# Edge products of a graph layer: two columns per product through a block-diagonal weight, and the bias as a bf16 product

## What is computed

```
e = edge_feats @ W_e + b_e                 # 200000 x 64 times 64 x 128, plus the bias
m = relu(e + node_feats[src])              # a gathered row of x for every edge
agg = segment_sum(m, dst, num_segments=n)
h = agg + (1.0 + eps) * node_feats
z = relu(batch_norm(h @ W1 + b1))
x = layernorm(x + z @ W2 + b2)
```

## Time and profile before

| | |
|---|---|
| median of 3 runs | 3382.34 us (3381.54 to 3385.09) |
| span of the profiled execution | 3381.6 us |
| edge loop (first window's addition to the last) | about 66 to 2360 us |
| PE busy | 2729.1 us, 81% |
| PE weight loads busy | 2301.2 us, 68% |
| DVE busy | 2217.4 us, 66% |
| ACT busy | 1611.3 us, 48% |
| POOL busy | 1526.4 us, 45% |

### The profile page before, as it was taken

The page is one execution under the profiler, slowest core; times in us unless marked ns, Lnnn a source line. Parts: engine busy times, 40 slices in busy tenths (PEclk is TensorE's granted clock), DMA queues, the critical chain, the costliest instruction groups (busy, mean ns, idle before and its releaser), DMA issues.

```text
span 3381.6 us, 49409 instructions
## 1 busy us (share of the span) xinstructions
PE 2729.1 (81%) x16231; PEld 2301.2 (68%) x16231; DVE 2217.4 (66%) x4031; ACT 1611.3 (48%) x2900; POOL 1526.4 (45%) x1641
## 2 busy tenths in 40 slices
PE   4777777777777777777777778777799999999995
PEld 3666666666666666666666667666578888888884
DVE  7676666666666666666666666667778874445445
ACT  3444444444444444444444444444555554445443
POOL 6666666666666666666666666664200000000000
PEclk9767777777777777777777776777899999999998
DMA  5333333333333333333333333333323333333333
GB/s 196 106 109 110 110 109 108 109 111 112 111 109 109 108 111 112 109 112 109 108 109 112 112 110 110 109 108 98 119 98 126 149 122 127 144 138 138 127 139 96
DMA packets 145445, 394.75 MB, mean 117 GB/s; under 512 B 36829, under 2 KB 100153, under 8 KB 139817
## 3 DMA queue, kind: packets, MB, share of 16 engines
q1 hardware_dynamic: 93356, 278.06, 22.3%
q0 software_dynamic: 50176, 102.50, 13.2%
q10 hardware_dynamic: 1662, 10.97, 0.8%
HBM read 286.59 MB, written 104.80 MB: 116 GB/s over the span
## 4 chain that ended last, share of the span: by engine, by line
PE 41%; DVE 31%; another core or an unknown queue 15%; issue 9%; ACT 2%; DMA 2%; DVEq 0%; SPq 0%; POOL 0%; ACTq 0%
DVE z L1148 13%; PE psE L1008 12%; PE psA L1008 12%; PE psE L872 6%; PE psA L902 5%; DVE work L1136 4%; DVE work L1156 4%; DVE work L1155 4%; PE psS L886 3%; DVE onehot L1142 3%; DMA work<-in_edge_cols 1%; PE psA L979 1%; ACT wide L810 0%; PE psA L948 0%
## 5 line engine op out<-in xcount | busy, mean ns | idle before, releaser
L683 POOL DMA_INDIRECT work<-in_x_flat,idx x1568 | 1492.7, 952 | 837.6 <-issue 421.6
L872 PE MATMUL psE<-we,work 65*128 65x128 f32 x3136 | 707.2, 357 | 555.8 <-issue 500.4
L872 PEld LDWEIGHTS psE<-we,work 65*128 65x128 f32 x3136 | 563.6, 248 | 656.8 <-issue 627.2
L736 ACT ACTIVATE z<-psA 128x490 int32 x392 | 227.0, 579 | 1215.1 <-PE psA L902 612.7
L1148 DVE TENSOR_SCALAR z<-iota_r,key,scale 128x490 bf16<-128x490 f16 x1568 | 716.0, 520 | 0.0
L902 PE MATMUL psA<-z 128*128 128x245 bf16 x3136 | 658.1, 386 | 2.4 <-issue 2.3
L1160 DVE TENSOR_TENSOR acc<-psS,acc 128x144 f32 x196 | 60.4, 308 | 757.3 <-remote 756.7
L742 ACT ACTIVATE z<-iota_c,low 128x128 bf16<-128x128 f16 x1568 | 476.9, 390 | 0.0
L886 PEld LDWEIGHTS psS<-onehot,work 128*128 128x128 f32 x3136 | 446.5, 226 | 11.3 <-issue 3.1
L1008 PE MATMUL psE<-wide,halves 128*128 128x500 f32 (+1 forms) x2058 | 448.4, 376 | 5.8 <-ACT halves L819 5.4
L902 PEld LDWEIGHTS psA<-z 128*128 128x128 bf16 x3136 | 366.0, 136 | 124.4 <-issue 3.9
(11 more groups left out here) (165 smaller groups left out, 1792.8 us busy)
## 6 DMA issues: line engine op xcount, KB each, us to landing
counts<-adjacency SPq DMA_DIRECT2D x36, 3062.5 KB, 9.6
adjacency<-work SPq DMA_DIRECT2D x392, 245.0 KB
work<-in_edge_cols SPq DMA_DIRECT2D x196, 256.0 KB
work<-in_x_flat,idx POOLq DMA_INDIRECT x1568
counts<-adjacency SPq DMA_DIRECT2D x3, 1592.5 KB, 6.2
acc<-in_x_cols ACTq DMA_DIRECT2D x1, 3136.0 KB
xn<-in_x_rows ACTq DMA_DIRECT2D x1, 3136.0 KB, 31.3
x_spill<-xn SPq DMA_DIRECT2D x12, 256.0 KB, 2.2
```

Of the source, the lines that this page charges most:

```text
L683: gp.indirect_dma_start(gath[0:size(g), g % R, j, :], None, x_flat[:, :], bass.IndirectOffsetOnAxis(ap=idx[0:size(g), g, j:j + 1], axis=0) ...
L736: act.activation(taken[:, w % TAKEN, :, :], ring[:, bass.ds(at, 2 * HC)].rearrange("p (a n) -> p a n", a=ODD), ACT.Copy).then_inc(evac_ok, 1)
L872: mm = pe.matmul(psE0[0:n, j, :], eaT[0:FE + 1, g % RE, j, 0:n], we[:, :], start=True, stop=True)
```

## The change

Two columns of the edge features are now stacked on the 128 partitions (64 features each), so that `eaT` holds 4 pairs instead of 8 columns. The weight becomes a block-diagonal matrix of 128 x 256: the product of a pair yields the 128 outputs of its first column and the 128 of its second. The bias no longer is a 65th row. For each of the two PSUM banks one bf16 product of all-ones with `edge_bias` (128 x 512) writes it first, and two fp32 products of 256 columns are added on top. `edge_bias` holds b_e split exactly into three bf16 parts in its rows 0, 1 and 2, repeated four times, and zeros below; DVE makes it at the start from a broadcast load `be`. The edge product is one function for both forms of the loop.

```
-        we = sb("we", [FE + 1, F])
+        we = sb("we", [2 * FE, 2 * F])
+        edge_bias = sb("edge_bias", [P, 4, F], BF16)
+        be = sb("be", [P, 2, F])
+        be_parts = sb("be_parts", [P, 3, F], BF16)
...
-        eaT = work[:, 4096:4096 + RE * J * P].rearrange("p (r j e) -> p r j e", r=RE, j=J)
+        eaT = work[:, 4096:4096 + RE * HP * P].rearrange("p (r j e) -> p r j e", r=RE, j=HP)
...
-            sp.dma_start(eaT[0:FE, g % RE, :, :], edge_cols[g, :, :, :]).then_inc(ea_in[g % RE], 16)
+            sp.dma_start(eaT[:, g % RE, :, :], edge_cols[g, :, :, :]).then_inc(ea_in[g % RE], 16)
...
+        def edge_columns(pe, slot, n):
+            for half in range(2):
+                pe.matmul(psE0[0:n, 4 * half:4 * half + 4, :].rearrange("p j f -> p (j f)"), ones_b[:, 0:n],
+                          edge_bias[:, :, :].rearrange("p j f -> p (j f)"), start=True, stop=True)
+                for q in range(2 * half, 2 * half + 2):
+                    mm = pe.matmul(psE0[0:n, 2 * q:2 * q + 2, :].rearrange("p j f -> p (j f)"), eaT[:, slot, q, 0:n], we[:, :],
+                                   start=False, stop=True, skip_group_check=True)
+            return mm
...
+            act.dma_start(be[:, 0, :], be_row.partition_broadcast(P)).then_inc(be_in, 16)
             act.dma_start(we[:, :], we_rows[:, :]).then_inc(we_in, 16)
...
-            def edge_product(g, j0, j1):
-                n = size(g)
-                if j0 == 0:
-                    pe.wait_ge(ea_in[g % RE], 16 * (g // RE + 1))
-                    if g >= 1:
-                        pe.wait_ge(sum_ok, g)
-                for j in range(j0, j1):
-                    mm = pe.matmul(psE0[0:n, j, :], eaT[0:FE + 1, g % RE, j, 0:n], we[:, :], start=True, stop=True)
-                if j1 == J:
-                    mm.then_inc(edge_mm, 1)
+            def edge_product(g):
+                pe.wait_ge(ea_in[g % RE], 16 * (g // RE + 1))
+                if g >= 1:
+                    pe.wait_ge(sum_ok, g)
+                edge_columns(pe, g % RE, size(g)).then_inc(edge_mm, 1)
...
             pe.wait_ge(we_in, 16)
-            edge_product(0, 0, J)
-            edge_product(1, 0, J)
+            pe.wait_ge(edge_bias_ok, 1)
+            edge_product(0)
+            edge_product(1)
...
-            link(ve.memset(eaT[FE:FE + 1, :, :, :], 1.0))
+            ve.wait_ge(be_in, 16)
+            link(ve.tensor_copy(be_parts[:, 0, :], be[:, 0, :]))
+            link(ve.tensor_tensor(be[:, 1, :], be[:, 0, :], be_parts[:, 0, :], ALU.subtract))
+            link(ve.tensor_copy(be_parts[:, 1, :], be[:, 1, :]))
+            link(ve.tensor_tensor(be[:, 1, :], be[:, 1, :], be_parts[:, 1, :], ALU.subtract))
+            link(ve.tensor_copy(be_parts[:, 2, :], be[:, 1, :]))
+            link(ve.tensor_scalar(be[:, 1, :], be_parts[:, 0, :], ident[:, 0:1], None, ALU.mult))
+            for part in (1, 2):
+                link(ve.scalar_tensor_tensor(be[:, 1, :], be_parts[:, part, :], ident[:, part:part + 1], be[:, 1, :],
+                                             ALU.mult, ALU.add))
+            ve.tensor_copy(edge_bias[:, :, :], be[:, 1, :].unsqueeze(1).to_broadcast([P, 4, F])).then_inc(edge_bias_ok, 1)
```

More of the change, by code:

```diff
@@ L54, in cdiv, with build @@
     return -(-a // b)
-def build(nc, E, x_flat, x_rows, x_cols, src_slots, src_chunks, dst_rows, dst_slots, dst_chunks, edge_cols, we_rows, par_cols,
+def build(nc, E, x_flat, x_rows, x_cols, src_slots, src_chunks, dst_rows, dst_slots, dst_chunks, edge_cols, we_rows, be_row, par_cols,
           w1_rows, w2_rows, wg_rows, b2_row, out):
     N, F = out.shape
-    FE = edge_cols.shape[1]
+    FE = edge_cols.shape[1] // 2
     H = w1_rows.shape[1]
@@ L219, in build @@
         we_in = sem("we_in")
+        be_in = sem("be_in")
+        edge_bias_ok = sem("edge_bias_ok")
         cols_par_in = sem("cols_par_in")
@@ L433, in body @@
                 part = edge_cols[bass.ds(g, 1), :, :, :].rearrange("a k j p -> k (a j p)")
-                sp.dma_start(eaT[0:FE, 0, :, :].rearrange("k j p -> k (j p)"), part).then_inc(sem_s["ea"], 16)
+                sp.dma_start(eaT[:, 0, :, :].rearrange("k j p -> k (j p)"), part).then_inc(sem_s["ea"], 16)
             general_groups(sp, body)
@@ L450, in body @@
                 pe.wait_ge(sem_s["ea"], 16 * g + 16)
-                for j in range(J):
-                    mm = pe.matmul(psE0[0:n, j, :], eaT[0:FE + 1, 0, j, 0:n], we[:, :], start=True, stop=True)
-                mm.then_inc(sem_s["prod"], 1)
+                edge_columns(pe, 0, n).then_inc(sem_s["prod"], 1)
                 pe.wait_ge(sem_s["msg"], g + 1)
@@ L920, in _ @@
                 if s + 2 < G:
-                    edge_product(s + 2, 0, J)
+                    edge_product(s + 2)
                 for i in range(HP):
@@ L1417 @@
                 dst_chunks=dst.reshape(-1, P).T,
-                edge_cols=attr.reshape(groups, P, J, -1).transpose(0, 3, 2, 1),
-                we_rows=np.concatenate([weight["L0_gnn_W_e"], weight["L0_gnn_b_e"][None]]),
+                edge_cols=attr.reshape(groups, P, J // 2, -1).transpose(0, 3, 2, 1),
+                we_rows=np.block([[weight["L0_gnn_W_e"], np.zeros_like(weight["L0_gnn_W_e"])],
+                                  [np.zeros_like(weight["L0_gnn_W_e"]), weight["L0_gnn_W_e"]]]),
+                be_row=weight["L0_gnn_b_e"],
                 par_cols=np.concatenate([weight[k].reshape(-1, P).T for k in ("L0_gnn_b1", "L0_gnn_gamma", "L0_gnn_beta",
```

## The result

The changed kernel takes 3369.56 us (median of 5 runs, 3367.93 to 3371.29) against 3382.34 us, a ratio of 0.9963 with a 95% interval of 0.9952 to 0.9973: 12.8 us faster, 0.4 us below the range of the prediction and on the side to which it had given 0.16. A second pair of medians under the same condition gave 0.9964 (e10). Under another condition, found in the experiments, the kernel before takes 3045 us and the change gains nothing: it was 0.25% slower in one pair (e5).

What follows compares the result with a forecast made beforehand. POOL's chain of eight gathers and some 2.1 us of waiting was taken to bound the loop. Span 3381.6 + 0 + 0.5 (start) + 0.7 (median over span) = 3382.8, rounded 3383 us; range 3370 to 3425.

Steps and rivals of the forecast that it cites:

- POOL's chain sets the period, PE does not: Edge loop: POOL's eight gathers plus some 2.1 us of waiting set the step of about 11.8 us, not PE.
- No burst, no hold: Edge loop: where POOL's gathers stand still or have ended, PE's edge product runs unbroken, in 3.75 or 1.94 us.
- The edge product, "I take 0": Edge loop: PE's work grows 0.2 to 0.6 us a step but lies under 4.7 us of hold, so 0 us.
- the hold: Edge loop: stretch in which PE issues nearly one record at a time and `win_mm` arrives 4.7 us late.
- rival 1: The hold depends on PE's instruction form or number: one 0.7 us break less per step, 134 us, 3249 us; chance 0.15.
- Sizes of the product: Edge product on PE: 2.1 us for 1.9 at the high clock, 4.3 for 3.75 at the low one.
- Rival 2: PE sets the loop's period and the longer edge product costs 38 to 115 us, 3421 to 3498 us; chance 0.07.
- 4.7 us of hold: Edge loop: time `win_mm` comes late at DVE after the window's end on PE, taken as cover for the edge product.
- The edge transfer, 0: Edge feature load: same 256 KB on 128 partitions; landing 1 us earlier or later only moves the product's start, 0 us.
- The start, +0.5: Before the loop: 2.9 us of added DVE operations are covered by idle time; POOL's chain moves -1 to +2, taken +0.5 us.
- The end, 0: Loop end and after: DVE awaits no edge product, later instructions are the same; clock phase -2.8 to +2, taken 0 us.
- The signs of being right: Trace: bursts every 11.8 us after 2.1 us idle, DVE idle about 4 us, product 2.1 to 4.3, first addition about 66.

Runs made afterwards that it cites:

- e10: The changed kernel itself on another chip, against the kernel before, with the hold: 0.9964 (kernel before 3382.25 us).
- e5: The changed kernel itself once more, against the kernel before, without the hold: 3051.84 for 3043.46 us, 1.0025.
- e8: The kernel before with seven gathers a step in place of eight from the fifth group on: 0.9209.
- e13: The changed kernel, edge product varied by 24-step stretches: eight narrow products, no bias, behind two or four chunk pairs, issued twice; 3376.60 us in one run.
- e16: The changed kernel, edge product in stretches of 36, 20 or 12 records and different forms: 3401.47 us, kernel before 3410.76 us, one run each.
- e12: The kernel before, varied by 24-step stretches: product moved, issued twice or three times, one column of eight, seven gathers; 3448.04 us in one run.
- e4: The kernel before with each edge product issued twice, without the hold: 0.9992 of a kernel before at 3045.6 us.
- e14: The changed kernel with two memsets of acc moved from POOL to ACT and a DVE sum moved to POOL behind the loop: 0.9964, without the hold.
- e15: The kernel before with two memsets of acc moved from POOL to ACT and a DVE sum moved to POOL behind the loop: 0.9966, without the hold.
- e6: The kernel before itself, run for its trace, without the hold: profiled span 3044.2 us, loop period 10.10 us.

## Why the prediction was wrong

**POOL's chain sets the period, PE does not: right.** e8 and the seven-gather stretch (10.44 for 11.83 us: one gather of 1.25 and 0.14 of the wait) show it under both conditions. "No burst, no hold" is weaker than it was put: the product read as unbroken in the earlier trace rows, at 171.78, runs while POOL gathers again, one every 1.25 us from 169.68 on. PE runs through the beginning of that burst and is held towards its end; only the product after POOL's last gather has no burst beside it.

**The edge product, "I take 0": this is the step that failed.** With the hold it was worth -11.0 us, 0.057 us in each of 192 steps: POOL's wait fell from 408.1 / 191 = 2.14 to 391.5 / 191 = 2.05 us, and the gathers took back 8 x 4 ns = 0.03. I treated what lies under the hold as free, as if its end were fixed by the burst alone. It follows the burst, but for forms like these it moves by 0.05 to 0.08 us with the number of PE's records in a step (e13, e16): eight narrow products, with everything else of the changed kernel, bring back 11.84 for 11.78 us. I had counted 20 for 32 records and put that into rival 1, but priced it there only in whole breaks of 0.7 us: the condition of rival 1 was right, its price twelve times too high, and between 0 and 134 us no case stood.

**Sizes of the product: right.** 2.1 us foreseen, 2.16 measured. That the wider stream does not matter was right as well, and the rule cited in the prediction, that the gap is columns over clock, described PE and missed the gain, which is not in PE's time: 36 and 20 records with the same columns differ by 0.06 us of the period (e13).

**Rival 2: rightly refused, but the cover was put too thick.** The longer product did not cost anything. But by "4.7 us of hold" another 1.9 us at the high clock should have been free, and twice the product costs 0.94 us a step with the hold (e12), against nothing without it (e4). In the changed kernel it costs 0.15 us (e13), and there the breaks have moved into the window.

**The edge transfer, 0: right as far as seen.** L405 waits for `edge_cols` in the trace, and the product starts elsewhere in the hold, as assumed; the transfer was not changed alone.

**The start, +0.5: wrong in sign.** The chain on DVE was sized well: `be` landed at 11.44 (10.3 to 12.65 foreseen), the nine operations took 3.1 us (2.9), and the next began 4.2 us late (2.7 to 5.9). The cover shrank from 10.75 to 1.36 us and held. But POOL's first gather started at 9.34 instead of 10.78 us, and the first addition came 1.0 us earlier, within the -1 to +2 that I gave. That is hardly the change's doing: the addition stands 55.2 us behind the first gather before and 55.6 us after, and in e12, whose start is that of the kernel before, the two are at 9.80 and 65.06 us. Why `idx` lands earlier in some executions was not tried.

**The end, 0: right** to 0.4 us. The loop's 11.0 us alone would have left the time at 3371.3 us, inside the range; start and end carried it out. The step would have failed all the same.

**The signs of being right could not tell.** Bursts every 11.77 us with 2.09 us before them, 3.92 us of DVE's idle time, a product of 2.16 us: all but the first window's addition (at 64.96 for about 66 us) are as foretold. A shift of 0.06 us a step is below what they were stated to.

**What no step foresaw** is that the hold is a condition of the run. The forecast named it as its weak point, that the trace doesn't show why a burst holds PE. The change gains 12.8 us with it and nothing without it: 1.0025 in e5, 0.9964 against 0.9966 in e14 and e15. What makes the hold stays open.

## What to carry to other kernels

Work that lies under a stall is free only if the stall's end does not depend on it; ask for the dependence in fractions of the stall, not in its whole quanta, since 0.06 us in each of 192 steps is 12 us. Where a stall has no cause in the trace, look at whether the trace itself is complete (unmatched senders, few semaphore events), and compare a second set of runs before tuning for it. Several forms in stretches of one program separate effects of 0.05 us a step that run-to-run spread hides; take the period from the engine that sets it, since another's steps can jump (12.02 for 11.92 us in e13).

## What the hardware showed unexpectedly

- The same kernel takes 3045 or 3382 us (3411 in one set), steady within a set of runs. With the hold PE's records come some 0.7 us apart, or twice that, in parts of POOL's bursts of indirect DMAs, and its last break ends about 1.7 us after the last gather (1016.09 and 1014.44 us); much of each burst runs unbroken. Ahead of the edge product's records such waits make 500.1 us of the loop with the hold and 0.5 us without it. The cause is open.
- With the hold the period moves with the number of PE's records in a step: +0.05 to +0.07 us for 36 in place of 20, whether fp32 or bf16, of 1 or of 128 columns.
- A gather of 0.94 us took 7.57 us under one DVE sum of two SBUF operands, and mostly 1.1 to 1.8 us where it met the one-hot and take-apart operations; in a loop that is POOL's chain this is 41 us of 3044 (sum of what e6's gathers exceed 0.945 us).
- 100 additions to a semaphore by SyncE in each step cost 41 us over 100 steps; PE then waited for the transfers queued behind them.
